# A graph network kernel: the index table, the order of the first transposes, and where groups of edge tiles begin

## What is computed

```
x  = _layernorm(x + _L0_gnn_ref(x, edge_index, W, b))     # out[dst] += (x W)[src] * norm
h  = gat_conv(x, edge_index, W1, ..., heads=4)            # softmax over the incoming edges
h  = relu(layer_norm(h)) + (x @ Wr1 + br1)
h2 = layer_norm(gat_conv(h, edge_index, W2, ..., heads=1)) + (h @ Wr2 + br2)
x  = _layernorm(x + h2)
```

## Time and profile before

| | |
|---|---|
| median of 3 runs | 1076.63 us (1074.85 to 1076.67) |
| the profiled execution | 1076.46 us |
| its span (first to last instruction) | 1074.7 us, mean granted TensorE clock 0.913 |
| TensorE busy | 872.0 us, 81% of the span |
| VectorE busy | 740.5 us, 69% |
| ScalarE, GpSimd busy | 325.0 us, 124.4 us |

### The profile page before, as it was taken

How to read it: one execution, slowest core, us unless ns; L and a number is a source line. 1 busy time by engine, 2 the same in 40 slices (tenths; PEclk the granted TensorE clock), 3 DMA queues, 4 the chain that set the end, 5 groups by cost and what they waited for, 6 DMA issues and landing times.

```text
span 1074.7 us, 14499 instructions
## 1 busy us (share of the span) xinstructions
PE 872.0 (81%) x4888; PEld 549.2 (51%) x4888; DVE 740.5 (69%) x1184; ACT 325.0 (30%) x523; POOL 124.4 (12%) x109
## 2 busy tenths in 40 slices
PE   2789888799679989948998259991889889899782
PEld 2456555456435434415887148881556456455441
DVE  6777778766735549886776978767565382388887
ACT  0323222400123211106662265644222100164430
POOL 4000000100000004321000520007230000000001
PEclk9899999899889999969999569995899899899886
DMA  6000000200371111313101100204111543201112
GB/s 243 1 1 1 1 1 1 74 1 0 104 322 40 40 50 59 127 53 123 42 25 63 59 1 25 78 0 142 49 60 59 216 136 138 88 1 59 59 59 85
DMA packets 22318, 72.18 MB, mean 67 GB/s; under 512 B 2562, under 2 KB 3306, under 8 KB 22014
## 3 DMA queue, kind: packets, MB, share of 16 engines
q1 hardware_dynamic: 19742, 61.01, 16.3%
q0 software_dynamic: 2528, 10.55, 2.8%
HBM read 51.22 MB, written 20.33 MB: 67 GB/s over the span
## 4 chain that ended last, share of the span: by engine, by line
PE 37%; issue 24%; DVE 13%; POOL 4%; DMA 2%; ACT 1%; POOLq 0%; ACTq 0%; DVEq 0%
PE psum L621 18%; PE psum L783 17%; DVE arena L1171 7%; POOL arena L541 1%; POOL arena L537 1%; DVE arena L1292 1%; POOL arena L573 1%; DMA arena<-as_scratch 1%; ACT arena L854 1%; DVE arena L1135 1%; DVE arena L1181 1%; DVE arena L1262 1%; PE psum L720 1%; DVE arena L1296 1%; POOL arena L494 1%
## 5 line engine op out<-in xcount | busy, mean ns | idle before, releaser
L621 PE MATMUL psum<-arena 128*128 128x512 f16 x2040 | 395.7, 355 | 27.8 <-DVE arena L993 16.4
L621 PEld LDWEIGHTS psum<-arena 128*128 128x128 f16 (+1 forms) x2040 | 202.0, 100 | 205.5 <-issue 19.4
L854 ACT ACTIVATE arena<-psum 128x320 f16<-128x320 f32 (+5 forms) x160 | 102.1, 675 | 425.7 <-PE psum L621 231.8
L783 PE MATMUL psum<-arena 128*128 x800 | 178.5, 385 | 18.3 <-DVE arena L1276 11.3
L783 PEld LDWEIGHTS psum<-arena 128*128 128x128 f32 x800 | 153.5, 193 | 43.4 <-issue 21.6
L829 PE MATMUL psum<-arena 128*128 128x512 f16 x600 | 106.2, 341 | 15.7 <-DVE arena L1345 15.7
L854 ACT ACTIVATE arena<-arena 128x256 f16<-128x256 f32 (+3 forms) x92 | 56.8, 632 | 174.7 <-PE psum L720 76.0
L1181 DVE CUSTOM_DVE_ANT_0 arena<-psum,arena 128x256 bf16<-128x256 f32 (+1 forms) x100 | 46.7, 527 | 85.6 <-ACT arena L854 85.6
L1171 DVE CUSTOM_DVE_ANT_0 arena<-arena 128x1280 bf16<-128x1280 bf16 x50 | 88.2, 1825 | 13.4 <-DMA arena<-as_scratch 13.4
L829 PEld LDWEIGHTS psum<-arena 128*128 128x128 f16 x600 | 60.7, 101 | 61.2 <-issue 22.6
L1273 DVE TENSOR_TENSOR arena<-arena 128x640 f32<-128x640 f32 x80 | 66.8, 835 | 28.9 <-ACT arena L935 28.9
(11 more groups left out here) (156 smaller groups left out, 642.4 us busy)
## 6 DMA issues: line engine op xcount, KB each, us to landing
arena<-in_L_gnn_W_dram SPq DMA_DIRECT2D x14, 384.0 KB, 4.9
r_scratch<-arena SPq DMA_DIRECT2D x10, 512.0 KB, 2.6
arena<-uv_scratch SPq DMA_DIRECT2D x16, 320.0 KB, 3.8
arena<-r_scratch SPq DMA_DIRECT2D x10, 512.0 KB, 4.0
x_scratch<-arena SPq DMA_DIRECT2D x10, 384.0 KB, 12.4
arena<-x_scratch SPq DMA_DIRECT2D x10, 384.0 KB, 3.5
r_scratch<-arena SPq DMA_DIRECT2D x10, 384.0 KB, 2.6
arena<-r_scratch SPq DMA_DIRECT2D x10, 384.0 KB, 4.0
```

The costliest lines, as they stand in the source:

```text
L621: ins = pe.matmul(o[:, a:b], part[:, k, ds(t * P, P)], w[:, k, a:b], start=(k == 0 and n == 0 and m == 0), stop=(k == kn - 1 and n == 1))
L783: last = pe.matmul(p_att[:, j, 0:HID + 1], pf[k % PSLOTS][:, j * P:(j + 1) * P], xl_f[:, k, ds(h, 1), 0:HID + 1].rearrange("p a n -> p (a ...
L854: act.activation(out_, in_, ACT.Copy, scale=scale).then_inc(signal, 1)
```

## The change

- GpSimd makes one of the four parts of `key_io` and makes it first, then `lo_io`, `thr` and `t_io`, and the identity after those. VectorE makes the other three parts by adding 32, 64 and 96, ahead of its wait for the transposed keys.
- TensorE transposes node tiles 0 and 1 ahead of its wait for the block ranges (`ranges_f`) instead of behind it.
- `key_s` and `lo_s` hold the keys twice: from the first edge tile on, and again from the second one on. The first tile is not rounded down any more; an odd one is read from the second copy, which lies 330 elements on (`odd * (ETP - 1) + first`). The shift of the keys works on 660 elements instead of 330.
- The doubled keys lie where the last of the `low_counts` are written later; so `low_counts` and `degrees` of node tiles 7, 8 and 9 come behind the loop (before: 8 and 9), and in the loop `low_counts` moves from behind the second block of a node tile to behind the third.

```diff
-IOTAS = 7 + SUBS
+IOTAS = 8
+TAIL = 3
...
-        lo_s = at(late_pos + T * WD * 2, [ETP], i16)
-        key_s = at(125 * KB, [ETP], i16)
+        lo_s = at(late_pos, [2 * ETP], i16)
+        key_s = at(88 * KB, [2 * ETP], i16)
...
@@ gpsimd
+            pool.iota(key_io[:, 0].rearrange("p (k w) c -> p k w c", k=T), [[KS, T], [1, WD], [0, 2]], base=0,
+                      channel_multiplier=0).then_inc(S["iotas"], 1)
+            pool.iota(lo_io, [[1, P], [0, 2]], base=0, channel_multiplier=0).then_inc(S["iotas"], 1)
...
-            for j in range(SUBS):
-                pool.iota(key_io[:, j].rearrange("p (k w) c -> p k w c", k=T), [[KS, T], [1, WD], [0, 2]], base=j * WD,
-                          channel_multiplier=0).then_inc(S["iotas"], 1)
@@ tensor
+            transposes(0)
+            transposes(1)
+            pe.wait_ge(S["ranges_f"], 1)
...
-            transposes(0)
-            transposes(1)
             project_nodes(0, range(KD))
...
-                    if j == 2 and 1 <= t < T - 1:
+                    if j == 2 and 1 <= t <= T - TAIL:
                         degrees(t - 1)
-            degrees(T - 2)
-            degrees(T - 1)
+            for t in range(T - TAIL, T):
+                degrees(t)
@@ vector
+            dve.wait_ge(S["iotas"], 1)
+            for j in range(1, SUBS):
+                dve.tensor_scalar(key_io[:, j], key_io[:, 0], float(j * WD), None, ALU.add).then_inc(S["dve"], 1)
             dve.wait_ge(S["keys_tr"], 1)
-            dve.tensor_copy(key_s, p_key[:, 0:ETP]).then_inc(S["dve"], 1)
-            dve.tensor_copy(lo_s, p_lo3[:, 0:ETP]).then_inc(S["dve"], 1)
+            for shift in range(2):
+                dve.tensor_copy(key_s[:, shift * ETP:(shift + 1) * ETP], p_key[:, shift:shift + ETP]).then_inc(S["dve"], 1)
+                dve.tensor_copy(lo_s[:, shift * ETP:(shift + 1) * ETP], p_lo3[:, shift:shift + ETP]).then_inc(S["dve"], 1)
...
-            dve.tensor_scalar(first_t, first_t, 2 ** 15 - 2, None, ALU.bitwise_and).then_inc(S["dve"], 1)
...
-            dve.tensor_tensor(range_i[:, 0:NB], first_t, g_latest, ALU.min).then_inc(S["dve"], 1)
+            dve.tensor_tensor(first_t, first_t, g_latest, ALU.min).then_inc(S["dve"], 1)
...
+            dve.tensor_scalar(odd, first_t, 1, None, ALU.bitwise_and).then_inc(S["dve"], 1)
...
+            dve.scalar_tensor_tensor(range_i[:, 0:NB], odd, float(ETP - 1), first_t, ALU.mult, ALU.add).then_inc(S["dve"], 1)
...
-                    if j == 1 and 1 <= t < T - 1:
+                    if j == 2 and 1 <= t <= T - TAIL:
                         low_counts(t - 1)
...
-            low_counts(T - 2)
-            low_counts(T - 1)
+            for t in range(T - TAIL, T):
+                low_counts(t)
```

More of the change, by code:

```diff
@@ L155, in gnn_program @@
         assert T * NP * 2 == 25 * KB
-        assert (T * WD + ETP) * 2 <= 16 * 10 * T and pos >= late_pos + 16 * 10 * T
-        zero_h = at(late_pos, [T * WD], f16)
-        lo_s = at(late_pos + T * WD * 2, [ETP], i16)
-        key_s = at(125 * KB, [ETP], i16)
+        assert 4 * ETP <= 16 * 10 * T and pos >= late_pos + 16 * 10 * T
+        zero_h = at(125 * KB, [T * WD], f16)
+        lo_s = at(late_pos, [2 * ETP], i16)
+        key_s = at(88 * KB, [2 * ETP], i16)
         ring_key = [at(4 * KB + i * G * T * WD * 2, [GP, T * WD, 2], f16) for i in range(2)]
@@ L186, in gnn_program @@
         g_latest = at(30 * KB + 640, [NB], i32, 1)
+        odd = at(30 * KB + 800, [NB], i32, 1)
         wst0 = [at((70 + 3 * i) * KB, [D], f32) for i in range(KD)]
@@ L456, in _ @@
             pool.memset(dst_i[:, 2, :], PAD_DST).then_inc(S["pads"], 1)
+            loose = dict(channel_multiplier=0, allow_small_or_imprecise_dtypes=True)
+            pool.iota(key_io[:, 0].rearrange("p (k w) c -> p k w c", k=T), [[KS, T], [1, WD], [0, 2]], base=0,
+                      channel_multiplier=0).then_inc(S["iotas"], 1)
+            pool.iota(lo_io, [[1, P], [0, 2]], base=0, channel_multiplier=0).then_inc(S["iotas"], 1)
+            for c in range(2):
+                pool.iota(thr[:, c:c + 1], [[0, 1]], base=c * WD, channel_multiplier=WD,
+                          allow_small_or_imprecise_dtypes=True).then_inc(S["iotas"], 1)
+            pool.iota(t_io, [[1, EG * P]], base=0, **loose).then_inc(S["iotas"], 1)
             pool.memset(ident, 0.0).then_inc(S["ident_ok"], 1)
@@ L462, in _ @@
                                    pattern=[[-1, P + shift]], channel_multiplier=1).then_inc(S["ident_ok"], 1)
[L463 to L467, removed]
             pool.memset(x_sb[:, T - 1, :], 0.0).then_inc(S["pads"], 1)
-            pool.iota(lo_io, [[1, P], [0, 2]], base=0, channel_multiplier=0).then_inc(S["iotas"], 1)
-            for j in range(SUBS):
-                pool.iota(key_io[:, j].rearrange("p (k w) c -> p k w c", k=T), [[KS, T], [1, WD], [0, 2]], base=j * WD,
-                          channel_multiplier=0).then_inc(S["iotas"], 1)
             pool.memset(zero_h, 0.0).then_inc(S["iotas"], 1)
@@ L596, in _ @@
             last.then_inc(S["tile_rows"], 1)
[L597 to L600, removed]
             def transposes(t):
@@ L612, in transposes @@
                 last.then_inc(S["x_tr"], 1)
+            transposes(0)
+            transposes(1)
+            pe.wait_ge(S["ranges_f"], 1)
+            for c in range(2):
+                last = pe.matmul(p_rng[:, c * NB:(c + 1) * NB], span[:, c:c + 1], ident[0:NB, 0:NB], start=True, stop=True)
+            last.then_inc(S["ranges_t"], 1)
             def product(o, lhs, rhs, t, kn, width, ks=None):
@@ L1007, in _ @@
             dve.tensor_reduce(tmm[:, 1, :], dst_f, axis=AX.X, op=ALU.max).then_inc(S["keys_prep"], 1)
+            dve.wait_ge(S["iotas"], 1)
+            for j in range(1, SUBS):
+                dve.tensor_scalar(key_io[:, j], key_io[:, 0], float(j * WD), None, ALU.add).then_inc(S["dve"], 1)
             dve.wait_ge(S["keys_tr"], 1)
-            dve.tensor_copy(key_s, p_key[:, 0:ETP]).then_inc(S["dve"], 1)
-            dve.tensor_copy(lo_s, p_lo3[:, 0:ETP]).then_inc(S["dve"], 1)
-            steps_done(2)
+            for shift in range(2):
+                dve.tensor_copy(key_s[:, shift * ETP:(shift + 1) * ETP], p_key[:, shift:shift + ETP]).then_inc(S["dve"], 1)
+                dve.tensor_copy(lo_s[:, shift * ETP:(shift + 1) * ETP], p_lo3[:, shift:shift + ETP]).then_inc(S["dve"], 1)
+            steps_done(SUBS + 3)
             dve.wait_ge(S["tile_rows"], 1)
@@ L1038, in _ @@
             first_t, end_t = range_t[:, 0:NB], range_t[:, NB:2 * NB]
-            dve.tensor_scalar(first_t, first_t, 2 ** 15 - 2, None, ALU.bitwise_and).then_inc(S["dve"], 1)
-            dve.wait_ge(S["dve"], steps_done(1))
             dve.tensor_tensor(groups, end_t, first_t, ALU.subtract).then_inc(S["dve"], 1)
@@ L1051, in _ @@
             steps_done(1)
-            dve.tensor_tensor(range_i[:, 0:NB], first_t, g_latest, ALU.min).then_inc(S["dve"], 1)
+            dve.tensor_tensor(first_t, first_t, g_latest, ALU.min).then_inc(S["dve"], 1)
+            dve.wait_ge(S["dve"], steps_done(1))
+            dve.tensor_scalar(odd, first_t, 1, None, ALU.bitwise_and).then_inc(S["dve"], 1)
+            dve.wait_ge(S["dve"], steps_done(1))
+            dve.scalar_tensor_tensor(range_i[:, 0:NB], odd, float(ETP - 1), first_t, ALU.mult, ALU.add).then_inc(S["dve"], 1)
             dve.wait_ge(S["dve"], steps_done(1))
@@ L1078, in one_hots @@
                 dve.reg_load(r1, range_i[0:1, b + NB:b + NB + 1])
-                first, end = dve.snap(r0, min_val=0, max_val=ETP - G), dve.snap(r1, min_val=G, max_val=ETP)
+                first, end = dve.snap(r0, min_val=0, max_val=2 * ETP - G), dve.snap(r1, min_val=G, max_val=2 * ETP)
                 with dve.Fori(first, end, G) as tile:
-                    g = nc.s_assert_within(tile, 0, ETP - G, skip_runtime_bounds_check_because="the loop ends at ETP at most, in steps of G from its start")
+                    g = nc.s_assert_within(tile, 0, 2 * ETP - G, skip_runtime_bounds_check_because="the loop ends at 2 ETP at most, in steps of G from its start")
                     def pairs(v, width):
```

## The result

The changed kernel took 1045.1 us (median of 5 runs, 1044.33 to 1046.21) against 1076.63, a ratio of 0.9713 (95% interval 0.97 to 0.9727), 31.5 us less. The forecast was 1045.8 us. The profiled execution has a span of 1043.1 us, 31.6 less than before.

What follows compares the result with a forecast made beforehand. TensorE was taken to bound ordinary counting tiles, with engines taking turns at two-group blocks, and a late chain the front end. Gains of 5.8 us (front end) and 24.9 us (counting) summed to 30.7, giving 1045.8 us, range 1043.9 to 1047.7.

Steps and rivals of the forecast that it cites:

- The groups: Counting stage: 44 groups become 40, gaining 21.4 us for four blocks with two groups, 5.3 each.
- The wait at the third block: Counting stage: moving `low_counts` removes TensorE's 0.43 us wait for one-hots in each tile, 3.0 us.
- It just fits: Next tile's first block: VectorE's one-hots end at 68.98, before TensorE arrives at 69.06.
- new waits at a tile's first block: Counting stage: TensorE waiting at each tile's first block was named as a sign of a wrong prediction.
- VectorE is late: Counting rival, chance 0.15: shift or moved `low_counts` exceeds 0.08 us of room; +3.4 us, 1049.2.
- The front end by GpSimd: Front end: GpSimd loses three of four tables, so the cast ends at 6.69, 5.30 us earlier.
- GpSimd holds VectorE up for less: Front-end rival, chance 0.10: the cast runs at once, 1.3 us more gained, 1044.5 us.
- in the trace the cast slipped in at none of the ends of the tables: Front end: the reason given for taking 5.30 us rather than 1.3 us more.
- The transposes: Front end: x transposed ahead of the ranges, so VectorE's waits before its two `xt_low` go, 0.73 us gained.
- The range arithmetic: Front end: one small instruction goes and two come, 0.2 us lost.
- The projection left as it is: Front end: the first projection's 7.73 us, partly at the low clock, were taken as unchanged.
- What was costed at nothing: VectorE's additions and PSUM copies, the loop's end, new SBUF places: hidden in waits or without effect, so nothing.

Runs made afterwards that it cites:

- x4: The changed kernel with `low_counts` behind the second block again instead of the third; 1046.94 us, ratio 0.9734.
- x6: The changed kernel with `low_counts` behind the second block and ahead of `xt_low`; 1043.14 us, ratio 0.9699.
- x10: The kernel before with GpSimd waiting for its own last table ahead of each of the four tables, opening small gaps; 1073.38 us, ratio 0.9979.
- x1: The kernel before with only the index table's part: one table by GpSimd, made first, three additions by VectorE; 1069.53 us, ratio 0.9945.
- x8: The changed kernel with GpSimd's work in the old order, its one table at its old place; 1046.46 us, ratio 0.9728.
- x2: The kernel before with only node tiles 0 and 1 transposed ahead of the ranges; 1075.86 us, ratio 1.0003.
- x7: The kernel before with GpSimd's work in the changed order but all four tables, made first; 1072.44 us, ratio 0.9972.
- x3: The kernel before with only the doubled keys, groups beginning at any tile, and `low_counts` and `degrees` as changed; 1054.56 us, ratio 0.9809.
- x9: x6 with GpSimd's fill of the last node tile and all behind it held until VectorE has made the keys; 1043.47 us, ratio 0.9707.

## Why the prediction was right

By its steps:

- **The groups** (21.4 us of the sum). Right in cause and size: 40 rows, each still 1.82 us. x4 has `low_counts` where the kernel before has it, and takes 21.8 us less for the counting (128.6 against 150.4), the 0.5 for degrees included. With rounding put back in the changed kernel it is 22.5 in the counting, more than the 21.4 of the sum.
- **The wait at the third block** (3.0 us). Right that it goes, but mis-sized: against x4 the move gained 1.4 us, and only x6, where VectorE isn't late, gains 3.2 (111.8 from tile 1's first block to tile 9's, against x4's 115.0). The row of 0.57 stands in six tiles of the kernel before, not in seven (tile 2, with two groups in its second block, lacks it), and VectorE was then late elsewhere. "It just fits" was the step that failed. The room at the next tile's first block was 0.08 us by the sum, and VectorE came later than that: L652 starts 0.28 us behind L648 at 61.57 where 0.14 is free of waits, and 0.64 at 76.22. These are the new waits at a tile's first block that the prediction named as a sign of being wrong; all of tiles 2 to 8 have one. From tile 1's first block to tile 9's it took 113.6 us (160.76 - 47.17) where 111.9 were forecast. x6 took 111.8 (159.33 - 47.54), so the sum for TensorE was right and the 1.7 us are VectorE's. The rival "VectorE is late", forecast at 3.4 us, came true at half its price. One part of it can be named: behind `xt_low` now stands a loop's entry, and the one-hots start 1.03 us behind it (50.67 to 51.70) where `low_counts` had started 0.87 behind (58.29 to 59.16 before). In two tiles VectorE also had 1.41 us and not 1.04 ahead of its first one-hots; why is open.
- **The front end by GpSimd** (5.30 us). The cause is shown by x10 and x1. The size was 6.2: the cast ended at 5.29, not 6.69, so the rival "GpSimd holds VectorE up for less" came true; the fill of L473 then took 0.5 us back. The failed step is "in the trace the cast slipped in at none of the ends of the tables", from which I took GpSimd's total work for the measure and gave its order no weight. x8, with one table in the old place, ends the cast at 6.71, as that sum has it. What counts is which instruction runs when the edges arrive, and whether a gap is near. Here the cast came at 4.86, just behind the 0.16 us gap ahead of L471.
- **The transposes** (0.73 us): VectorE's step from the end of its ranges to W0's remainders shrank by 0.9 us. In x2's time alone this can't be told from nothing. The range arithmetic lost 0.2 us, as forecast. TensorE's small matmuls ahead of it were 0.4 us faster than before in this trace (L595 2.50 us against 2.78, L613 0.30 against 0.42), which the sum did not have.
- **The projection left as it is**: it was 0.4 us shorter by the clock granted in this run (7.21 from start to first block, against 7.57); the prediction had no reason for that, and no run here gives one.
- **What was costed at nothing** (additions, copies, the loop's end, the new places) cost nothing: from tile 9's first block to L1122 it is 171.55 - 160.76 = 10.8 us, and before from 191.58 to the same copy at 202.37 also 10.8.

The sum was 30.7 against 31.5 measured: 1.8 us too little in the front end and 1.7 too much in the counting nearly cancel, and 0.8 us lie behind the counting, less than the spread of the runs. So the total is closer than its terms, and that is luck: two rivals came true in part, one each way.

On the lock for a whole instruction that the Trainium skill describes ("SBUF — State Buffer", section "Who interferes with whom"): x7 and x10 agree, one VectorE instruction at a table's end. The kernel before doesn't: its cast came at 4.92, passed the ends of all four tables, and ended at 11.99, 0.34 us behind the fill that follows them (11.30 to 11.65); the same in x2 (4.62) and x3 (4.83). In x8 it passed one end and a fill. Why a waiting cast gets in between two tables in x7 and not in these is open; at x10's gaps the waiting instruction got in each of three times.

## What to carry to other kernels

Where two engines share a ring with a fixed slot for each block, a block that needs one group more costs both engines' time for it one after the other, and the clock behind the wait besides: here 5.3 to 6 us for a group of 2.6; count such blocks from the data before tuning either engine. Long GpSimd fills at a kernel's start are cheap only if VectorE has no simple copies or scalar operations then; put them ahead of the data's arrival, or leave gaps, as far as these kernels show. And when a wait is removed from an engine that bounds, look at the next place where the other one is due: an operation put ahead of a wait that exists anyway (x6) costs nothing, while one put behind it was late again.

## What the runs showed of the hardware

- VectorE's copy or one-input scalar operation of 0.36 us took up to 7.4 us (x2, 4.62 to 11.99) beside back-to-back GpSimd tables, and 0.85 beside a fill that had started first (0.41 where it started behind, x6); an operation with two inputs beside a table took its usual 0.56 (x10, L1005).
- GpSimd is held up too: its fill of 768 took 0.94 us beside VectorE's shift (L473 in the changed kernel) and 0.73 alone (L468 in the kernel before).
- The first projection, the same 36 matmuls, took 7.2 to 8.6 us in different kernels with granted clocks of 0.81 to 0.67, so a start that is 0.4 us earlier can end 0.5 us later (x9).
